# DLRM tower with a compressed interaction network: SBUF tensors placed at multiples of 2048 bytes, weight tensors at multiples of 512 bytes behind them

## The reference

```python
e = stack([tbl_f[ids[:, f]] for f in range(32)], axis=1)      # (512, 32, 64)
def layer(hidden, x, w, b):                                   # w: (128, H*32)
    z = einsum('bhd,bfd->bhfd', hidden, x).reshape(B, H * 32, 64)
    return relu(einsum('bcd,oc->bod', z, w) + b)
y0 = layer(e, e, w0, b0);  hidden, direct0 = y0[:, :64], y0[:, 64:]
y1 = layer(hidden, e, w1, b1)
z = concatenate([direct0, y1], axis=1).sum(-1)                # (512, 192)
h = concatenate([z, dense_ctx], axis=1)
out = relu(relu(h @ W_top1 + b_top1) @ W_top2 + b_top2) @ W_top3
```

## Time and profile before

| | |
|---|---|
| median of 3 runs | 1057.91 us (1057.24 to 1058.9) |
| the profiled execution's own time | 1057.96 us |
| its span in the trace | 1056.2 us |
| TensorE busy | 1014.5 us, 96% of the span |
| VectorE busy | 932.9 us, 88% |
| GpSimd busy | 915.6 us, 87% |
| ScalarE busy | 792.9 us, 75% |
| granted TensorE clock | 1.00, the 2.4 GHz level |

### The profile page before, as it was taken

How to read it: one execution, slowest core, us unless ns; L and a number is a source line. 1 busy time by engine, 2 the same in 40 slices (tenths; PEclk the granted TensorE clock), 3 DMA queues, 4 the chain that set the end, 5 groups by cost and what they waited for, 6 DMA issues and landing times.

```text
span 1056.2 us, 11554 instructions
## 1 busy us (share of the span) xinstructions
PE 1014.5 (96%) x3561; PEld 670.2 (63%) x3561; DVE 932.9 (88%) x806; ACT 792.9 (75%) x951; POOL 915.6 (87%) x310
## 2 busy tenths in 40 slices
PE   2399999999999999999999999999999999999999
PEld 1146566566666666666666666666666666666663
DVE  3089999999999999999999999999999999999981
ACT  5057666678788878887888788878887887788772
POOL 6519877889999999999999999999998989898980
DMA  6498888878788877888788788787766776777620
GB/s 173 93 235 188 192 190 184 196 180 185 188 184 189 191 188 181 190 183 189 181 196 185 177 189 191 183 182 186 189 167 167 171 185 168 165 177 188 157 72 0
DMA packets 140832, 184.20 MB, mean 174 GB/s; under 512 B 55697, under 2 KB 56337, under 8 KB 140642
## 3 DMA queue, kind: packets, MB, share of 16 engines
q1 hardware_dynamic: 136178, 179.19, 71.9%
q0 software_dynamic: 4096, 4.20, 2.6%
q10 hardware_dynamic: 496, 0.06, 0.0%
HBM read 174.92 MB, written 8.39 MB: 174 GB/s over the span
## 4 chain that ended last, share of the span: by engine, by line
PE 93%; issue 3%; SPq 1%; DMA 1%; POOL 1%; DVE 0%; ACT 0%
PE py L795 34%; PE py L805 16%; PE py L804 16%; PE py L816 16%; PE py L825 3%; PE py L831 3%; PE py L824 2%; PE py L836 1%; POOL emb L402 1%; DMA xs<-x_dram 1%; SPq L347 0%; DVE zf L681 0%; SPq L302 0%; PE pzB L895 0%; PE pzS L895 0%
## 5 line engine op out<-in xcount | busy, mean ns | idle before, releaser
L413 POOL TENSOR_TENSOR zl<-zf,zh 128x2048 fp32r<-128x2048 f32 x178 | 788.0, 4433 | 83.0 <-ACT zh L481 81.0
L681 DVE TENSOR_TENSOR zf<-xs,hid 128x2048 f32<-128x2048 f32 (+1 forms) x256 | 536.9, 2105 | 42.7 <-ACT hid L511 40.3
L481 ACT ACTIVATE zh<-zf 128x1536 fp32r<-128x1536 f32 (+1 forms) x184 | 338.1, 1837 | 75.5 <-DVE zf L681 72.3
L795 PE MATMUL py<-zf,wf 128*128 128x512 f32 x860 | 391.0, 592 | 2.3 <-DVE zf L681 2.3
L804 PE MATMUL py<-zh,wh 128*128 128x512 f32 x736 | 291.5, 396 | 0.0
L805 PE MATMUL py<-zh,wl 128*128 128x512 f32 x736 | 291.0, 395 | 0.0
L795 PEld LDWEIGHTS py<-zf,wf 128*128 128x128 f32 x860 | 162.7, 189 | 158.1 <-issue 141.7
L816 PE MATMUL py<-zl,wh 128*128 128x512 f32 x736 | 228.6, 432 | 0.0
L816 PEld LDWEIGHTS py<-zl,wh 128*128 128x128 f32 x736 | 138.6, 188 | 59.6 <-issue 28.9
L804 PEld LDWEIGHTS py<-zh,wh 128*128 128x128 f32 x736 | 138.3, 188 | 33.7 <-issue 0.2
L805 PEld LDWEIGHTS py<-zh,wl 128*128 128x128 f32 x736 | 138.3, 188 | 33.6 <-issue 0.2
(11 more groups left out here) (104 smaller groups left out, 649.3 us busy)
## 6 DMA issues: line engine op xcount, KB each, us to landing
xs<-x_dram SPq DMA_DIRECT2D x512, 256.0 KB
xs<-x_dram SPq DMA_DIRECT2D x252, 64.0 KB
xt_pair<-x_dram SPq DMA_DIRECT2D x128, 64.0 KB
x_pair<-x_dram SPq DMA_DIRECT2D x128, 64.0 KB
x_dram<-emb SPq DMA_DIRECT2D x66, 64.0 KB
x_dram<-emb SPq DMA_DIRECT2D x22, 96.0 KB
emb<-in_tbl,idx POOLq DMA_INDIRECT x128
x_dram<-emb SPq DMA_DIRECT2D x4, 384.0 KB
```

The lines of the kernel that those rows point to most:

```text
L413: pool.tensor_tensor(zl[:, q, first:T], zf[:, s, first:T], zh[:, q, first:T].bitcast(F32), ALU.subtract).then_inc(lo["P"], 1)
L481: act.activation(zh[:, q, first:T], zf[:, s, first:T], ACT.Copy).then_inc(hi, 1)
L681: dve.tensor_tensor(zf[:, slot(u), first:T], left[:, first:T], view(right, at, [[0, T - first], [1, N]]), ALU.mult).then_inc(mult, 1)
L795: mm = pe.matmul(y, wf[:, w, h], zf[:, s, h], start=first and h == first_tile, stop=ends and h == T - 1)
```

## The change

The calls of `sb(...)` are put in another order, and one tensor `pad` of 64 bytes, which nothing reads or writes, is added. The small tensors come first, `pad` fills up to a multiple of 2048, then the data tensors whose sizes are multiples of 2048 follow, then `sums1` and `spreads` (1024 and 3072 bytes), and the weight tensors, whose 128-column tiles have 512 bytes, come last. No instruction is added, removed or moved: on every engine the program has the same instructions in the same order; lines behind the allocations have a number higher by 2 (L795 is L797).

```diff
-        emb = sb("emb", [P, 2, F, D])
         idx = sb("idx", [P, NC, F], I32)
-        wh = sb("wh", [P, len(SPLIT_NAMES), T, P], F32R)
-        wl = sb("wl", [P, len(SPLIT_NAMES), T, P], F32R)
-        wf = sb("wf", [P, len(WHOLE_NAMES), T, P])
-        whB = sb("whB", [P, len(OWN), P], F32R)
-        wlB = sb("wlB", [P, len(OWN), P], F32R)
-
-        wS = sb("wS", [P, 2, P], F32R)
-        pair16 = sb("pair16", [P, 2, 16], F32R)
-        low_rows = sb("low_rows", [P, 1])
         ident = sb("ident", [P, P])
+        dense = sb("dense", [P, NC, 16])
+        turns = sb("turns", [F, 2 * F])
         bias0 = sb("bias0", [P, 1])
         bias1 = sb("bias1", [P, 1])
+        wt3 = sb("wt3", [P, 2])
+        bt1 = sb("bt1", [P, 4])
+        bt2 = sb("bt2", [P, 2])
+        low_rows = sb("low_rows", [P, 1])
+        pair16 = sb("pair16", [P, 2, 16], F32R)
+
+        pad = sb("pad", [P, 16])
+        emb = sb("emb", [P, 2, F, D])
         xs = sb("xs", [P, 3 * T + 1, N])
...
-        sums1 = sb("sums1", [P, B // 2])
...
-        turns = sb("turns", [F, 2 * F])
-        spreads = sb("spreads", [P, T + 2, P])
...
         wt2 = sb("wt2", [P, 4, 256])
-        wt3 = sb("wt3", [P, 2])
-        bt1 = sb("bt1", [P, 4])
-        bt2 = sb("bt2", [P, 2])
-        dense = sb("dense", [P, NC, 16])
+        sums1 = sb("sums1", [P, B // 2])
+        spreads = sb("spreads", [P, T + 2, P])
+        wh = sb("wh", [P, len(SPLIT_NAMES), T, P], F32R)
+        wl = sb("wl", [P, len(SPLIT_NAMES), T, P], F32R)
+        wf = sb("wf", [P, len(WHOLE_NAMES), T, P])
+        whB = sb("whB", [P, len(OWN), P], F32R)
+        wlB = sb("wlB", [P, len(OWN), P], F32R)
+
+        wS = sb("wS", [P, 2, P], F32R)
```

## The result

The changed kernel takes 1043.13 us (median of 4 runs, 1043.07 to 1043.47) against 1057.74 us for the kernel before beside it; the ratio is 0.9862 with a 95% interval of 0.9847 to 0.9876. The prediction said 1057.5 us, in a range of 1050 to 1062.

A forecast was written before the change was run, and what follows sets the result against it. The prediction took TensorE's own pace to bound the kernel from 77 to 1030 us. Its terms, 0 + 0 + 0 + 0 - 0.4 us, gave a median of 1057.5 us, range 1050 to 1062.

The forecast's parts named there:

- What bounds the kernel: From 77 to 1030 us only TensorE's own pace counts; other engines or transfers can reach the end only before 77 us.
- fp32 at 0: TensorE's fp32 stream: about 429 to 430 ns per instruction from three addresses, so the new placement costs 0.
- Weight loads at 0: TensorE's weight loads: 188 and 189 ns, covered by matmuls of 233 ns or more, so costed at 0.
- fp32r at 0: TensorE's 2614 fp32r matmuls: called the unknown, bounded by 49 us gain or as much loss, taken as 0.
- rival C: TensorE: load and stream at distance 0 collide, slowing fp32r; 1062 to 1070 us, or 1107 us at worst; chance 7%.
- A: TensorE: fp32r streams faster, saving up to 18.6 ns per matmul; 1028 us, 1020 to 1040; chance 14%.
- The second support: fp32r on TensorE: weight tiles start at four places mod 2048, yet 16 matmuls through two units' tiles keep one pace.
- A's cap by GpSimd: Groups 11 to 42: TensorE's period falls to 14.38 us, but GpSimd holds it at 14.68, leaving about 0.3 us.
- The text's own test: Step between fp32r matmuls: 233 ns if the prediction holds, 216 or so for faster streaming, above 233 for a collision.
- Transfers, 0.4 us: Loads of `xs` ahead of 77 us: faster loads worth 0 to 0.84 us of VectorE's wait, middle taken.
- the ninth that the prediction had estimated: Loads of `xs`: 8 transactions instead of 9 by the skill's rule, shortening them by up to a ninth, 0.9 us.

The follow-up runs named there:

- e7: Changed kernel plus extra matmuls, 16 to a line, between warm-up and loop, varying data and weight places, column counts and fp32; its total time says nothing.
- e10: Changed kernel with 32 bytes of padding ahead of `wh`: weights at 32 mod 512, data still at 0 mod 2048; 1057.63 us.
- e14: Kernel before with the weights alone moved by 224 bytes, to 352 mod 512, data left where they were; 1044.65 us, ratio 0.987.
- e13: Changed kernel with all weights moved 128 bytes further, to 128 mod 512, data at 0 mod 2048; 1057.58 us.
- e9: Changed kernel plus a grid of extra fp32r matmuls, 24 to a line, varying data and weight places and weight columns; its total time says nothing.
- e11: Changed kernel with 32 bytes of padding ahead of `emb`, so that data and weights are both at 32; 1044.33 us.
- e12: Changed kernel plus extra fp32r matmuls, 32 to a line, weights at 0 and data at 0 to 320 bytes; its total time says nothing.
- e1: Kernel before with 32 bytes of padding ahead of `xs`: data at 384 mod 2048, weights still at 128 mod 512; 1043.71 us, ratio 0.9869.

## Why the prediction was wrong, point by point

**What bounds the kernel.** Right, and what made the rest so simple: between 77 us and the end of the loop TensorE is busy 937 of 937 us. From 77 us on every ns of its pace showed in the time.

**fp32 at 0.** Right: 6.87 us for 16 fp32 instructions before and after, and e7 has 6.87 from six starting places.

**Weight loads at 0.** The duration is right, 188 ns before and after. The reason given for the 0 isn't: the text let a load cost nothing as long as it is shorter than the stream beside it. Moving the weights alone takes the whole gain away (e10) or gives it (e14), with loads of 188 ns each time.

**fp32r at 0.** This is the step that failed: "The nearest row is the fp32 stream, which reads the same bytes of the same kind of tensor and doesn't mind its address, so I take 0." The fp32 stream doesn't mind its address, but it takes its columns at half the pace, and its insensitivity carries nothing over to fp32r. The text had said so itself under rival C and yet gave C and A together 21%. What the runs showed in place of the 0 is a step of 226.7 ns instead of 233.3, set by the distance between data and weights. The second support was worse. "The weight side does vary", it said of tiles at 640, 1152, 1664 and 128. They vary by multiples of 512, and the pace has a period of 256 (e13, e9): four tiles, but one distance. The evidence had no variation in what mattered.

**The size, and rival A.** Rival A, with a chance of 14%, had the right effect: fp32r matmuls became faster. It took the whole excess of 18.6 ns per matmul, 49 us of TensorE work. The mean step fell by 5.45 ns, 13.5 us over 2481 steps; 12.0 ns of the 18.6 stay at the best distance (e7). At that size nothing changes hands: the period, 14.95 us, stays above GpSimd's 14.68, so A's cap by GpSimd, worked out for 14.38 us, never came into play. 1028 us was 15 us too far. The text's own test knew only 216 ns for A and more than 233 for C; 226.7 lies between.

**Rival C, a collision of load and stream at distance 0.** The right quantity with the wrong sign. It named the distance between the two operands, which no other part of the prediction did, and distance 0 is the best place (e9, e11, e14). The rule that it was weighed against, two separate read ports ("TensorE: Matmul & The Clock Gate" of the Trainium skill, section "Step-by-step: what each phase is for"), would make the distance of no account; e10 and e11, with the same values in data and weights and a distance of 224 and of 0, are 13 us apart.

**Transfers, 0.4 us.** The direction is shown, the 0.4 us isn't. This timeline of the changed kernel answers to the earlier trace rows: VectorE waits 0.58 us for `xs` (0.84 before), and TensorE waits only at 61.87, which is ScalarE's doing, and no longer at about 73 us.

```profile
61.87 7.13 PE L797 MATMUL py<-zf,wf 128*128 128x512 f32 x16 [1.53 <-DVE zf L683]
...
68.16 6.68 DVE L683 TENSOR_TENSOR zf<-xs,hid 128x2048 f32<-128x2048 f32 x3 [0.58 <-DMA xs<-x_dram]
```

The line of the queue that loads `xs` (packets, MB, time of its packets as a share of 16 engines' span), of before, of the changed kernel and of e4, in which `emb` and the weights have their places of the changed kernel and the data tensors stand 32 bytes further:

```profile
q1 hardware_dynamic: 136178, 179.19, 71.9%
```

```profile
q1 hardware_dynamic: 136178, 179.19, 70.2%
```

```profile
q1 hardware_dynamic: 136178, 179.19, 72.2%
```

Times the span these are 759, 731 and 762 us for the same packets. The six kernels with `xs` at a multiple of 256 bytes have 728 to 743 us (changed, e7, e9, e10, e12, e13), the ten others 752 to 767. So transfers do mind the place, by 4% between before and changed and not by the ninth that the prediction had estimated. VectorE's wait near 68 us is 0.20 to 0.58 us in those six and 0.53 to 0.94 in the ten. At the end of the kernel this can't be told from the spread of single runs: the first `wl`-`zh` matmul starts at 76.5, 77.2 and 78.1 us in the changed kernel, e10 and e13, and at 76.7 to 78.6 in the ten. That the stretch ahead of it became 1.0 us shorter in this pair of traces is in part luck.

**What stays open.** The runs show that the pace goes by the distance, with a period of 256 bytes, and not why. Which weights meet the stream, the matmul's own or those that are loaded for the next one, can be read from the starts where one line of e7, e9 or e12 gives way to the next after a row of steps of 226 to 227 ns. Where the next matmul takes its weights from a place at another distance from the running stream, the last step of the old line already takes 232 to 237 ns (seven changes; from L871 to L872 in e9 it is 235). Where the weights stay and only the next matmul's data move, it still takes 226 to 227 (six changes; from L883 to L884 in e9 it is 227). So it is the load for the next matmul that costs the running stream. Each of these is a single step, an eighth change, to a load of 32 columns, stays at 226, and a matmul without a load wasn't tried. Nor is it shown why a few steps in the changed kernel stay at 236 ns, as from L838 to L818, which keep its mean of 227.9 above the 226.7 of the long rows, or why shorter streams don't pay for the distance (e7).

## What to carry to other kernels

Where a trace shows TensorE never waiting, compare the step between starts of each kind of matmul with its columns at the granted clock before anything else: a few ns each are the whole kernel's per cent. For fp32r matmuls of 512 columns, put data and weights at the same place mod 256 bytes; 32 bytes of padding at the right place were worth 1.3% here (e1), and alignment for its own sake nothing for TensorE (e10). And before a row is taken as evidence that an address doesn't matter, check that the addresses in it differ in the quantity that could matter, and that the instruction runs at the same pace as the one in question.

## What the runs showed of the hardware that I had not expected

- An fp32r matmul of 128x128 by 512 columns steps at 226.7 ns when data and weights have the same place mod 256 bytes, at 229 with 64 bytes between them, at 231 to 235 at the other multiples of 16 from 16 to 224, and at 237 with 4 bytes between them (e9, e12). 16 bytes below the same place (240) is as good as 0, 16 above it (16) is not: 7.26 against 7.41 us for 32.
- With 256 or 384 columns a distance of 32 bytes costs nothing: 117 and 173 ns against 120 and 174 at 0 (e7, L883 to L886).
- It is the load for the next matmul that costs the running stream: the last step before the weights change place takes 232 to 237 ns, before only the data do 226 to 227 (e7, e9, e12).
- An fp32 instruction of the same shape takes 429.4 ns from every place tried (e7).
- At distance 0, an fp32r matmul has 13 to 14 ns over one column per cycle at 2.4 GHz with 256, 384 and 512 columns alike (e7).
- Loading 32, 64 or 96 weight columns in place of 128 made the step longer and not shorter at distance 0, 5.53 to 5.54 us for 24 against 5.47 (e9, L888 to L890 against L893).
- The same packets of the queue that loads `xs` took 728 to 743 us of 16 engines' time with `xs` at a multiple of 256 bytes, 752 to 767 at other places (six and ten kernels).
